# One issuer instead of two for the first loads, and inputs laid out by tile and by chunk

## The chip, the cores and the metric

The kernel runs on one core of one Trainium2 chip. The metric is the device time of one execution in microseconds (us). The core has a matrix engine (TensorE, PE in the rows, its weight loads PEld), a vector engine (VectorE, DVE), a scalar engine (ScalarE, ACT), GpSimd (POOL) and SyncE (SP), which here only issues transfers. ACT can issue transfers too. Each of the two issuers has a queue of its own (q1 is SP's, q10 is ACT's), and both are served by the same 16 DMA engines.

## The reference

`x` is 16 batches of 128 x 128. A mixture of experts with a shared expert is added to it (8 routed experts, D = 128, F = 512), and then one matrix per batch, picked from a table of 100 by `fwd_steps`, is applied and added.

```python
g = jnp.einsum('bsd,edf->ebsf', h, Wg)
u = jnp.einsum('bsd,edf->ebsf', h, Wu)
expert_outs = jnp.einsum('ebsf,efd->ebsd', jax.nn.silu(g) * u, Wd)
expert_output = jnp.einsum('be,ebsd->bsd', gating_probs, expert_outs)
shared = jnp.einsum('bsf,fd->bsd', jax.nn.silu(h @ Sg) * (h @ Su), Sd)
sg = shared_gate_prob[:, :, None]
x = x + (1.0 - sg) * expert_output + sg * shared
x = x + jnp.einsum('bij,bjk->bik', T[fwd_steps - 1], x)
```

## The kernel before

The work is cut into steps. A step is one expert (9 with the shared one), one tile of 512 columns (4 batches; there are `NT` = 4 tiles) and one chunk of 128 of the 512 hidden features (`NC` = 4 chunks): 144 steps. Float32 accuracy is had by splitting each operand into a rounded high part and a low part (`x_hi`/`x_lo`, `w_hi`/`w_lo`, `h_hi`/`h_lo`) and adding three matmuls for each product. So a step has nine matmuls of 128 x 512: three for `g_bank` and three for `u_bank` (L378 to L380), and, two steps later (`LAG`), three for `o_bank` (L404, L405, L407). ACT takes `silu` of `g_bank` (L236) and rounds `h` (L242), DVE multiplies by `u_bank` (L295) and makes `h_lo` (L301). POOL splits the weights of the next expert (L168, L173) and adds the scaled results to `acc` (L218). Every engine has its program written out by hand; semaphores link them.

`w_raw` holds two experts (two slots). The first expert is loaded in parts, so that work can begin before all of it is there. In memory its row for a partition is 4 chunks of gate, up and down weights, 128 floats each. The start goes like this:

- SP issues tile 0 of `x` into `acc` (256 KB), then gate and up of chunks 2 and 3 (L132, 256 KB), then down of all four chunks (L133, 256 KB), then tile 1 of `x`, `side`, tiles 2 and 3 of `x`, and the second expert (L126, 768 KB).
- ACT issues gate and up of chunk 0 and of chunk 1 (L258, 128 KB each), `wc0_in[0]` and `wc0_in[1]` being their semaphores. Then it loads its table for silu and waits for the chunks in turn, rounding each (L255).
- DVE rounds tile 0 of `x` as soon as it is there (L329) and makes `x_lo` of it (L331), then `w_lo` of chunk 1 (L333), then rounds chunks 2 and 3 (L336).
- POOL makes `w_lo` of chunk 0, then of chunks 2 and 3, then of the down weights (all L168).
- PE runs six matmuls on zeros (L432), waits for `x_hi` and chunk 0, and runs the high products of chunk 0 and, once it is rounded, of chunk 1 (L438). Only then come the low products of both chunks (L441, L442), and then the steps from the third on, one behind the other. `project_down` of step 0 (L404) needs the low part of the down weights.

From the second expert on, a whole expert is loaded into the slot that POOL has just freed.

Of the kernel before, what the change touches and what calls it, by code (L numbers as in the profile page):

```python
# [12 lines left out]
def moe_then_step_kernel(  # L13
# [8 lines left out]

    S, B, D = out.shape
    E = W_all.shape[0] - 1
    NC = W_all.shape[2]
    K = TT.shape[0]
    assert S == P and D == P
    BT = 4
# [1 line left out]
    W = BT * S  # L30
    U = NT * NC
    N_ROUTED = E * U
# [5 lines left out]
    EARLY = 3  # L38
    assert NC == 4 and NT == 4 and E % 2 == 0

    with ExitStack() as ctx:
        def sb(name, shape, dt=F32):
            return ctx.enter_context(nc.sbuf_tensor(name, shape, dt))

        def sem(name):
            return ctx.enter_context(nc.semaphore(name))
# [3 lines left out]
        x_lo = sb("x_lo", [P, NT, W], F32R)  # L50
        w_raw = sb("w_raw", [P, 2, NC, 3, P])
        w_hi = sb("w_hi", [P, 2, NC, 3, P], F32R)
        w_lo = sb("w_lo", [P, 2, NC, 3, P], F32R)
        silu_g = sb("silu_g", [P, 2, W])
# [3 lines left out]
        acc = sb("acc", [P, NT, W])  # L58
# [15 lines left out]
        wc0_in = [sem(f"wc0_in{i}") for i in range(3)]  # L74
        wd0_in = sem("wd0_in")
        w_in = [sem(f"w_in{s}") for s in range(2)]
# [27 lines left out]
        parts = [(t * BT, BT) for t in range(NT - 1)] + [((NT - 1) * BT + b, 1) for b in range(BT)]  # L104
        last_part = len(parts) - 1
        parts_of = [[i for i, (b, _) in enumerate(parts) if b // BT == t] for t in range(NT)]

        def part_bank(i):

            b, nb = parts[i]  # L110
            return o_bank[(b // BT) % 2] if nb == BT else u_bank[b % BT]
# [3 lines left out]

        SCALE = [N_ROUTED + NC * t + NC + LAG for t in range(NT - 1)]
        TURN = [n + 1 for n in SCALE]
# [5 lines left out]
        @block.sync  # L123
        def _(sp):
            def load_expert(slot, e):
                sp.dma_start(w_raw[:, slot, :, :, :], W_all[e, :, :, :, :].rearrange("a p c m f -> (a p) c m f")).then_inc(w_in[slot], 16)  # L126

            def load_x(t0, t1, s):
                sp.dma_start(acc[:, t0:t1, :], xT[:, t0:t1, :]).then_inc(s, 16)

            load_x(0, 1, x_in[0])
            sp.dma_start(w_raw[:, 0, 2:NC, 0:2, :], W_all[0, :, 2:NC, 0:2, :]).then_inc(wc0_in[2], 16)  # L132
            sp.dma_start(w_raw[:, 0, :, 2, :], W_all[0, :, :, 2, :]).then_inc(wd0_in, 16)  # L133
            load_x(1, 2, x_in[1])
            sp.dma_start(side_b[:, :], side).then_inc(c_in, 16)
            load_x(2, NT, x_in[2])
            load_expert(1, slice(1, 2))

            sp.wait_ge(split_done, EARLY)
            with sp.Fori(1, E // 2) as pair:  # L140
                for slot in range(2):

                    sp.wait_ge(w_ready, 2 * NC * pair + NC * (slot - 1))
                    load_expert(slot, bass.ds(2 * pair + slot, 1))

            with sp.Fori(0, B) as b:
                which = sp.value_load(step[bass.ds(b, 1)].rearrange("(a n) -> a n", a=1), min_val=1, max_val=K)
                sp.dma_start(T_plus[:, bass.ds(b, 1), :], TT[bass.ds(which - 1, 1), :, :].rearrange("n j i -> j n i")).then_inc(T_in, 16)
            sp.wait_ge(w_ready, NC * (E - 1))
            load_expert(0, slice(E, E + 1))  # L150


            for first, last in [(i, i) for i in range(NT - 1)] + [(NT - 1, NT), (NT + 1, NT + 2)]:
                b0, b1 = parts[first][0], parts[last][0] + parts[last][1]
                sp.wait_ge(res_done, last + 1)
                sp.dma_start(out[:, b0:b1, :], res[:, b0:b1, :]).then_inc(stored, 16)
            sp.wait_ge(stored, 16 * (NT + 1))
# [72 lines left out]
        @block.scalar  # L230
        def _(act):
            def silu(n, k):


                act.wait_ge(g_done, n + 1)
                nc.scalar.activation(silu_g[:, k % 2, :], g_bank[k % 2][:, :], ACT.Silu).then_inc(g_read, 1)  # L236

            def round_h(n, k):


                act.wait_ge(h_done, n + 1)
                nc.scalar.activation(h_hi[:, k % HR, :], u_bank[k % HR][:, :], ACT.Copy).then_inc(h_rounded, 1)  # L242

            def copy_y(i):
                b, nb = parts[i]
                act.wait_ge(y_turned, i + 1)
                nc.scalar.activation(y[:, b:b + nb, :], part_bank(i)[:, 0:nb * D].rearrange("p (b d) -> p b d", b=nb),
                                     ACT.Copy).then_inc(y_done, 1)

            def round_x(t):  # L250
                act.wait_ge(x_in[min(t, 2)], 16)
                nc.scalar.activation(x_hi[:, t, :], acc[:, t, :], ACT.Copy).then_inc(x_rounded, 1)

            def round_w0(c, m):
                nc.scalar.activation(w_hi[:, 0, c, m, :], w_raw[:, 0, c, m, :], ACT.Copy).then_inc(w0_rounded, 1)  # L255

            for c in range(2):
                act.dma_start(w_raw[:, 0, c, 0:2, :], W_all[0, :, c, 0:2, :]).then_inc(wc0_in[c], 16)  # L258
            act.wait_ge(zero_done, 1)
            nc.scalar.activation(silu_0[:, :], zero[:, 0:1], ACT.Silu)  # L260
            for c in range(2):
                act.wait_ge(wc0_in[c], 16)
                round_w0(c, slice(0, 2))
            silu(0, 0)
            act.wait_ge(wd0_in, 16)
            round_w0(slice(0, NC), 2)
            silu(1, 1)
            round_h(0, 0)
            round_x(1)
            for n in range(2, PEEL_ACT):  # L270
                silu(n, n)
                round_h(n - 1, n - 1)

                if n >= PEEL_ACT - 2:
                    round_x(NT - PEEL_ACT + n)
            with act.Fori(0, N_ROUTED, U) as n0:
                for k in range(PEEL_ACT, U + PEEL_ACT):
                    silu(n0 + k, k)
                    round_h(n0 + k - 1, k - 1)
            for n in range(N_ROUTED + PEEL_ACT, N + 1):  # L280
                if n in COPY[:-1]:
                    copy_y(COPY.index(n))
                if n < N:
                    silu(n, n)
                round_h(n - 1, n - 1)
            for i in range(NT - 2, len(parts)):
                copy_y(i)
# [244 lines left out]
```

## Time and profile before

| | |
|---|---|
| median of 3 runs | 311.44 us (311.27 to 313.25) |
| the profiled execution | 311.43 us |
| its span, from the first to the last instruction | 309.6 us |
| around the span (the difference) | 1.83 us |
| PE busy | 303.3 us, 98% of the span |
| DVE, ACT, POOL busy | 214.0, 163.5, 102.5 us |
| granted TensorE clock, mean | 0.998 |
| moved by DMA | 10.39 MB, mean 34 GB/s |

The span is what the trace shows; the time outside it is not seen there. PE is busy nearly throughout, so the places to look at are the few microseconds in which it is not.

### The profile page before, as it was taken

What the parts mean: (1) busy time and instruction counts of PE and PEld (TensorE: products, weight loads), DVE (VectorE), ACT (ScalarE), POOL (GpSimd) and SP (SyncE); (2) the same over time, 40 slices, a digit from 0 to 9 for tenths busy, and PEclk for the clock granted to TensorE, in tenths of its full rate; (3) what the DMA queues carried; (4) which work ended last, traced back from release to release, by engine and by line L of the source; (5) the groups of instructions that cost most, each with busy time, mean ns of one, the idle gap of its engine ahead of it and who ended that gap; (6) DMA issues with size and microseconds to landing.
All of it is one profiled execution on the core that took longest, in us unless ns stands there. A gap on an engine that the chain in (4) does not pass through costs nothing.

```text
span 309.6 us, 4555 instructions
## 1 busy us (share of the span) xinstructions
PE 303.3 (98%) x1356; PEld 251.1 (81%) x1356; DVE 214.0 (69%) x348; ACT 163.5 (53%) x303; POOL 102.5 (33%) x116
## 2 busy tenths in 40 slices
PE   5999999999999999999999999999999999999995
PEld 4788888888888888888888888888888888888884
DVE  2667766777667666677766776667766676667785
ACT  2765555555555555555555555555555555554552
POOL 2675213441145115511551144312441155180000
PEclk9999999999999999999999999999999999999999
DMA  7600300020003000110003000012000000000011
GB/s 216 233 2 0 103 1 2 0 102 1 0 0 95 6 0 0 28 74 0 0 0 111 25 25 25 25 37 90 0 0 0 0 0 0 0 2 0 34 36 68
DMA packets 5847, 10.39 MB, mean 34 GB/s; under 512 B 592, under 2 KB 4048, under 8 KB 5840
## 3 DMA queue, kind: packets, MB, share of 16 engines
q1 hardware_dynamic: 5552, 10.04, 9.7%
q10 hardware_dynamic: 288, 0.26, 0.3%
q8 instruction: 4, 0.07, 0.1%
q14 instruction: 3, 0.02, 0.0%
HBM read 9.25 MB, written 1.05 MB: 33 GB/s over the span
## 4 chain that ended last, share of the span: by engine, by line
PE 97%; DMA 2%; DVE 0%; ACT 0%; ACTq 0%; issue 0%
PE o_bank L404 11%; PE o_bank L405 11%; PE o_bank L407 11%; PE g_bank L378 10%; PE u_bank L378 10%; PE g_bank L379 10%; PE u_bank L379 10%; PE g_bank L380 10%; PE u_bank L380 10%; DMA w_raw<-in_W_all 2%; PE o_bank L425 1%; PE o_bank L417 0%; DVE res L324 0%; PE u_bank L417 0%; PE g_bank L438 0%; PE g_bank L441 0%
## 5 line engine op out<-in xcount | busy, mean ns | idle before, releaser
L295 DVE TENSOR_TENSOR u_bank<-u_bank,silu_g 128x512 f32<-128x512 f32 x144 | 100.8, 700 | 85.9 <-PE u_bank L380 84.2
L236 ACT ACTIVATE silu_g<-g_bank 128x512 f32<-128x512 f32 x144 | 86.1, 598 | 133.8 <-PE g_bank L380 132.3
L301 DVE TENSOR_TENSOR h_lo<-u_bank,h_hi 128x512 fp32r<-128x512 f32 x144 | 98.0, 681 | 0.1
L218 POOL TENSOR_TENSOR acc<-acc,scaled 128x512 f32<-128x512 f32 x32 | 41.4, 1295 | 163.2 <-DVE scaled L309 163.0
L242 ACT ACTIVATE h_hi<-u_bank 128x512 fp32r<-128x512 f32 x144 | 85.5, 594 | 0.7 <-DVE u_bank L295 0.7
L404 PE MATMUL o_bank<-h_hi,w_hi 128*128 128x512 f32 x144 | 56.2, 391 | 0.0
L407 PE MATMUL o_bank<-h_lo,w_hi 128*128 128x512 f32 x144 | 56.1, 389 | 0.0
L405 PE MATMUL o_bank<-h_hi,w_lo 128*128 128x512 f32 x144 | 56.0, 389 | 0.0
L378 PE MATMUL g_bank<-x_hi,w_hi 128*128 128x512 f32 x142 | 55.6, 392 | 0.0
L380 PE MATMUL g_bank<-x_hi,w_lo 128*128 128x512 f32 x142 | 55.3, 389 | 0.0
L378 PE MATMUL u_bank<-x_hi,w_hi 128*128 128x512 f32 x142 | 55.3, 389 | 0.0
L379 PE MATMUL g_bank<-x_lo,w_hi 128*128 128x512 f32 x142 | 55.3, 389 | 0.0
L380 PE MATMUL u_bank<-x_hi,w_lo 128*128 128x512 f32 x142 | 55.2, 389 | 0.0
L379 PE MATMUL u_bank<-x_lo,w_hi 128*128 128x512 f32 x142 | 55.2, 389 | 0.0
L168 POOL TENSOR_TENSOR w_lo<-w_raw,w_hi 128x384 fp32r<-128x384 f32 (+2 forms) x36 | 36.3, 1011 | 7.8 <-ACT w_hi L255 4.6
L404 PEld LDWEIGHTS o_bank<-h_hi,w_hi 128*128 128x128 f32 x144 | 27.0, 188 | 5.8 <-POOL w_lo L168 0.3
L407 PEld LDWEIGHTS o_bank<-h_lo,w_hi 128*128 128x128 f32 x144 | 27.0, 188 | 5.8
L405 PEld LDWEIGHTS o_bank<-h_hi,w_lo 128*128 128x128 f32 x144 | 27.0, 188 | 5.5
L380 PEld LDWEIGHTS g_bank<-x_hi,w_lo 128*128 128x128 f32 x142 | 26.7, 188 | 5.6
L380 PEld LDWEIGHTS u_bank<-x_hi,w_lo 128*128 128x128 f32 x142 | 26.7, 188 | 5.6
L378 PEld LDWEIGHTS u_bank<-x_hi,w_hi 128*128 128x128 f32 x142 | 26.7, 188 | 5.6
L379 PEld LDWEIGHTS u_bank<-x_lo,w_hi 128*128 128x128 f32 x142 | 26.7, 188 | 5.5
(51 smaller groups left out, 145.2 us busy)
## 6 DMA issues: line engine op xcount, KB each, us to landing
w_raw<-in_W_all SPq DMA_DIRECT2D x8, 768.0 KB, 4.4
T_plus<-in_TT SPq DMA_DIRECT2D x16, 64.0 KB, 1.7
out_y<-res SPq DMA_DIRECT2D x3, 256.0 KB, 2.5
acc<-in_xT SPq DMA_DIRECT2D x2, 256.0 KB, 5.0
w_raw<-in_W_all SPq DMA_DIRECT2D x2, 256.0 KB, 5.4
acc<-in_xT SPq DMA_DIRECT2D x1, 512.0 KB, 6.0
w_raw<-in_W_all ACTq DMA_DIRECT2D x2, 128.0 KB, 4.9
out_y<-res SPq DMA_DIRECT2D x2, 128.0 KB, 2.4
```

Source lines behind the costliest of these rows:

```text
L168: return nc.gpsimd.tensor_tensor(w_lo[:, slot, c, m, :], w_raw[:, slot, c, m, :], w_hi[:, slot, c, m, :].bitcast(F32), ALU.subtract)
L218: nc.gpsimd.tensor_tensor(acc[:, t, :], acc[:, t, :], scaled[:, t % 2, :], ALU.add).then_inc(acc_done, 1)
L236: nc.scalar.activation(silu_g[:, k % 2, :], g_bank[k % 2][:, :], ACT.Silu).then_inc(g_read, 1)
L242: nc.scalar.activation(h_hi[:, k % HR, :], u_bank[k % HR][:, :], ACT.Copy).then_inc(h_rounded, 1)
L295: nc.vector.tensor_tensor(u_bank[k % HR][:, :], u_bank[k % HR][:, :], silu_g[:, k % 2, :], ALU.mult).then_inc(h_done, 1)
L301: nc.vector.tensor_tensor(h_lo[:, k % HR, :], u_bank[k % HR][:, :], h_hi[:, k % HR, :].bitcast(F32), ALU.subtract).then_inc(split_done, 1)
L378: nc.tensor.matmul(bank, w_hi[:, w[0], w[1], w[2], :], x_h, start=start, stop=False)
L379: nc.tensor.matmul(bank, w_hi[:, w[0], w[1], w[2], :], x_l, start=False, stop=False)
L380: return nc.tensor.matmul(bank, w_lo[:, w[0], w[1], w[2], :], x_h, start=False, stop=stop)
L404: nc.tensor.matmul(o_bank[t % 2][:, :], w_hi[:, w[0], w[1], w[2], :], h_hi[:, slot, :], start=c == 0, stop=False)
L405: nc.tensor.matmul(o_bank[t % 2][:, :], w_lo[:, w[0], w[1], w[2], :], h_hi[:, slot, :], start=False, stop=False)
L407: last = nc.tensor.matmul(o_bank[t % 2][:, :], w_hi[:, w[0], w[1], w[2], :], h_lo[:, slot, :], start=False, stop=c == NC - 1)
```

## The change

All loads of the start are now issued by SP, and chunk 0 and chunk 1 stand right behind tile 0 of `x`; ACT issues none. The arrays have another order in memory: `x` is stored as four tiles of 128 x 512, each contiguous (before, a partition's row held all four tiles, 8 KB, and a tile took 2 KB of each row). The weights of an expert are stored as four chunks, each 128 rows of gate, up and down (1.5 KB a row); before, a partition's row held all four chunks (6 KB). In the scratchpad nothing moves.

```diff
-    NC = W_all.shape[2]
+    NC = W_all.shape[1]
...
             def load_expert(slot, e):
-                sp.dma_start(w_raw[:, slot, :, :, :], W_all[e, :, :, :, :].rearrange("a p c m f -> (a p) c m f")).then_inc(w_in[slot], 16)
+                sp.dma_start(w_raw[:, slot, :, :, :], W_all[e, :, :, :, :].rearrange("a c p m f -> p (a c) m f")).then_inc(w_in[slot], 16)
 
             def load_x(t0, t1, s):
-                sp.dma_start(acc[:, t0:t1, :], xT[:, t0:t1, :]).then_inc(s, 16)
+                sp.dma_start(acc[:, t0:t1, :], xT[t0:t1, :, :].rearrange("t p w -> p t w")).then_inc(s, 16)
 
             load_x(0, 1, x_in[0])
-            sp.dma_start(w_raw[:, 0, 2:NC, 0:2, :], W_all[0, :, 2:NC, 0:2, :]).then_inc(wc0_in[2], 16)
-            sp.dma_start(w_raw[:, 0, :, 2, :], W_all[0, :, :, 2, :]).then_inc(wd0_in, 16)
+            sp.dma_start(w_raw[:, 0, 0, 0:2, :], W_all[0, 0, :, 0:2, :]).then_inc(wc0_in[0], 16)
+            sp.dma_start(w_raw[:, 0, 1, 0:2, :], W_all[0, 1, :, 0:2, :]).then_inc(wc0_in[1], 16)
+            sp.dma_start(w_raw[:, 0, 2:NC, 0:2, :], W_all[0, 2:NC, :, 0:2, :].rearrange("c p m f -> p c m f")).then_inc(wc0_in[2], 16)
+            sp.dma_start(w_raw[:, 0, :, 2, :], W_all[0, :, :, 2, :].rearrange("c p f -> p c f")).then_inc(wd0_in, 16)
...
-            for c in range(2):
-                act.dma_start(w_raw[:, 0, c, 0:2, :], W_all[0, :, c, 0:2, :]).then_inc(wc0_in[c], 16)
             act.wait_ge(zero_done, 1)
...
     def pack(gate, up, down):
         e = gate.shape[0]
-        g = gate.reshape(e, P_, NC_, P_)
-        u = up.reshape(e, P_, NC_, P_)
-        d = down.reshape(e, NC_, P_, P_).transpose(0, 2, 1, 3)
+        g = gate.reshape(e, P_, NC_, P_).transpose(0, 2, 1, 3)
+        u = up.reshape(e, P_, NC_, P_).transpose(0, 2, 1, 3)
+        d = down.reshape(e, NC_, P_, P_)
         return _np.stack([g, u, d], axis=3)
...
-        "xT": x.transpose(2, 0, 1).reshape(D_, 4, -1),
+        "xT": x.transpose(2, 0, 1).reshape(D_, 4, -1).transpose(1, 0, 2),
```

SP, from its first instruction to its loop over the experts, before. `in_xT` and `in_W_all` are the arrays in memory, `acc` and `w_raw` the tiles they go to:

```order
1 L129 DMA acc<-in_xT 128x512
2 L132 DMA w_raw<-in_W_all 128x2x256
3 L133 DMA w_raw<-in_W_all 128x4x128
4 L129 DMA acc<-in_xT 128x512
5 L135 DMA side_b<-in_side 128x144
6 L129 DMA acc<-in_xT 128x1024
7 L126 DMA w_raw<-in_W_all 128x1536
```

The same stretch of SP after the change:

```order
1 L129 DMA acc<-in_xT 128x512
2 L132 DMA w_raw<-in_W_all 128x256
3 L133 DMA w_raw<-in_W_all 128x256
4 L134 DMA w_raw<-in_W_all 128x2x256
5 L135 DMA w_raw<-in_W_all 128x4x128
6 L129 DMA acc<-in_xT 128x512
7 L137 DMA side_b<-in_side 128x144
8 L129 DMA acc<-in_xT 128x2x512
9 L126 DMA w_raw<-in_W_all 128x4x384
```

Two issues of 128 x 256 stand ahead of the rest, which keeps its order; an expert is now 128 x 4 pieces of 384 floats instead of 128 of 1536, and tiles 2 and 3 of `x` are two pieces a partition instead of one.

ACT, from its start, before:

```order
0 L230 UNCONDITIONAL_BRANCH
1 L258 DMA w_raw<-in_W_all 128x256 x2
2 L260 ACT_TABLE_LOAD
3 L260 ACTIVATE silu<-zero 128x1
4 L255 ACTIVATE w_hi<-w_raw 128x256 x2
```

ACT, after:

```order
0 L232 UNCONDITIONAL_BRANCH
1 L260 ACT_TABLE_LOAD
2 L260 ACTIVATE silu<-zero 128x1
3 L257 ACTIVATE w_hi<-w_raw 128x256 x2
4 L238 ACTIVATE silu_g<-g_bank 128x512
```

Only the two issues are gone from ACT. The instructions of PE, DVE and POOL are the same and in the same order.

## Rows read from the trace of the kernel before

**Rows 1.** The page: span, and busy time and share of PE.

```profile
span 309.6 us, 4555 instructions
PE 303.3 (98%) x1356; PEld 251.1 (81%) x1356; DVE 214.0 (69%) x348; ACT 163.5 (53%) x303; POOL 102.5 (33%) x116
```

**Rows 2.** The chain that ended last, 0 to 14 us: start, length, what.

```profile
0.74 0.41 ACTq L258
...
1.18 5.15 DMA w_raw<-in_W_all
...
6.35 0.43 ACT w_hi L255
...
6.82 0.50 PE g_bank L438
...
10.76 0.35 PE o_bank L404
```

**Rows 3.** Timeline of SP's queue, start: start, length, line.

```profile
0.74 0.39 SPq L129 DMA_DIRECT2D acc<-in_xT  x1
1.19 0.42 SPq L132 DMA_DIRECT2D w_raw<-in_W_all  x1
1.65 0.64 SPq L133 DMA_DIRECT2D w_raw<-in_W_all  x1
```

**Rows 4.** Timeline of ACT, DVE, POOL and PE to 11 us; in brackets, idle time before.

```profile
5.36 0.42 ACT L255 ACTIVATE w_hi<-w_raw 128x256 fp32r<-128x256 f32 x1 [2.20 <-DMA w_raw<-in_W_all]
8.55 0.62 ACT L255 ACTIVATE w_hi<-w_raw 128x512 fp32r<-128x512 f32 x1
10.02 0.64 ACT L252 ACTIVATE x_hi<-acc 128x512 fp32r<-128x512 f32 x1
...
5.17 0.43 DVE L329 CAST x_hi<-acc 128x512 fp32r<-128x512 f32 x1 [4.16 <-DMA acc<-in_xT]
...
5.86 1.05 POOL L168 TENSOR_TENSOR w_lo<-w_raw,w_hi 128x256 fp32r<-128x256 f32 x1 [4.38 <-ACT w_hi L255]
...
1.06 2.93 PE L432 MATMUL o_bank<-zero 128*128 128x128 f32 x12 [1.06 <-DVE zero L327]
5.92 0.47 PE L438 MATMUL g_bank<-x_hi,w_hi 128*128 128x512 f32 x1 [1.93 <-ACT w_hi L255]
7.38 0.40 PE L441 MATMUL g_bank<-x_lo,w_hi 128*128 128x512 f32 x1
```

**Rows 5.** Issues from 1.6 to 1.7 us: KB, median us to landing.

```profile
w_raw<-in_W_all SPq DMA_DIRECT2D x2, 256.0 KB, 5.4
```

**Rows 6.** Queues from 2 to 4 us, then 9 to 10: packets, MB, share of 16 engines.

```profile
q1 hardware_dynamic: 112, 0.21, 59.9%
q10 hardware_dynamic: 89, 0.09, 14.8%
...
q1 hardware_dynamic: 67, 0.37, 89.5%
```

**Rows 7.** Windows: length, PE, PEld, DVE, ACT, POOL, PEclk, DMA share, GB/s.

```profile
2.00:3.00 1.00, 1.00 (x7) 1.00 (x6) 0.00 (x0) 0.99 (x2) 0.00 (x0) 1.00 0.83 158
3.00:4.00 1.00, 0.99 (x5) 0.70 (x4) 0.00 (x0) 0.16 (x1) 0.00 (x0) 1.00 0.67 134
4.00:5.00 1.00, 0.00 (x0) 0.00 (x0) 0.00 (x0) 0.00 (x0) 0.00 (x0) 1.00 1.03 352
5.00:6.00 1.00, 0.08 (x1) 0.11 (x1) 0.80 (x2) 0.42 (x1) 0.14 (x1) 1.00 1.14 366
...
33.00:34.00 1.00, 1.00 (x6) 0.84 (x5) 0.54 (x1) 0.80 (x2) 0.00 (x0) 1.00 0.74 184
34.00:35.00 1.00, 1.00 (x6) 0.81 (x5) 1.00 (x3) 0.25 (x1) 0.00 (x0) 1.00 0.98 395
```

**Rows 8.** A later expert load: its issue, and POOL's first use of it.

```profile
31.91 0.34 SPq L126 DMA_DIRECT2D w_raw<-in_W_all  x1
...
52.98 0.51 POOL L173 CAST w_hi<-w_raw 128x384 fp32r<-128x384 f32 x1
```

## The prediction

> **What bounds the kernel now.** I read the page first [rows 1]: PE is busy for 303.3 of 309.6 us, so only some 6 us of the span can be had from anything but PE's own work, and the change leaves that work alone. The chain of waits [rows 2] says where those microseconds are. From 6.82 us on it is PE behind PE, except for one place: the first `o_bank` matmul takes 0.35 us of the chain instead of the 0.23 of its neighbours. Before 6.82 it goes back over ACT's rounding of chunk 1 to the transfer of chunk 1, issued at 1.18 us and 5.15 us under way. So the start is bound by loads, the other 302 us by PE. What the change gives or takes is how much earlier or later the unbroken run of PE begins; everything behind slides with it.
>
> The timeline [rows 4] shows the start. PE's matmuls on zeros are over at 3.99 us. `x_hi` waits for `x` until 5.17. ACT starts to round chunk 0 at 5.36, so it landed at about 5.27, PE starts at 5.92, and the pair of high products of chunk 1 at 6.82 (chunk 1 landed at 1.18 + 5.15 = 6.33). The low products begin at 7.38.
>
> **What a start needs.** Call the landing of chunk 0 A and of chunk 1 B. Two paths lead to the low products:
> - by chunk 1: B + 1.05 (7.38 - 6.33): rounding 0.42, two matmuls and the steps between.
> - by POOL's `w_lo` of chunk 0, which takes 1.05 and ended at 5.86 + 1.05 = 6.91 [rows 4], 1.64 behind A; with 0.05 to pass it on, A + 1.69. Before that was 6.96 and hidden under 7.38.
> The later of the two counts. `x` adds 0.43 + 0.69 for its high and low parts behind its landing and is hidden as long as it lands no later than A.
>
> **The change part by part.**
>
> *Issue.* An issue on SP takes 0.39 to 0.42 us, and the next starts 0.45 us behind it [rows 3]. Chunk 0 goes out at 1.19 instead of 0.74, chunk 1 at 1.64 instead of 1.18, chunks 2 and 3 and the down weights 0.9 later (2.1 and 2.55). This costs time only where a transfer would else have been moving data in those 0.45 us. By 4.0 the DMA engines are far behind what was issued (0.30 MB moved [rows 6] of the 1.05 MB of the first five loads), so the later issue is hidden by the backlog. Without that cover it costs 0.45 us at B and A.
>
> *Order in the queue.* Bytes moved, from the windows [rows 7]: 0.30 MB by 4 us, 0.35 MB more by 5, 0.37 MB more by 6, so 0.65 MB at 5.0 and 1.02 at 6.0. At A = 5.27 it was 0.75 MB, at B = 6.33 it was 1.14 MB. `x` and chunk 0 are 0.39 MB, with chunk 1 0.52 MB. So 0.36 MB of later loads (chunks 2 and 3, down) had been moved by A and 0.62 MB by B: two queues share the engines, and SP's brings what is needed later. In one queue these stand behind. Full credit, at 360 GB/s: A 1.0 earlier (4.3), B 1.7 earlier (4.6). The sum goes to max(4.3 + 1.69, 4.6 + 1.05) = 5.99, a gain of 1.4 us. Little credit: by 4.0 most of `x` (0.21 of 0.26 MB) had been moved, yet it landed at about 5.1; so some engines are late with `x` itself, and what stands behind it on those is not helped by the order. Then A stays near `x` at 5.1 and B follows at 128 KB behind it, 0.4 us, 5.5: max(6.79, 6.55) = 6.8, a gain of 0.6.
>
> *Layout of `x`.* From 2 to 4 us q1 moved 112 packets in 59.9% of 16 engines, 171 ns each, most of them of 2 KB. From 9 to 10 us, 67 packets with 0.37 MB (6 KB each, but for a few) took 89.5%, 214 ns each, so 71 ns for 2 KB [rows 6]. The first `x` is read at well under half speed. Whether its pitch of 8 KB in memory does that, the trace doesn't say directly. An expert load, which is one contiguous block before, is also slow at its start, 184 GB/s, but one microsecond later it runs at 395 [rows 7]; `x` and the chunks stay at 134 to 158 for two. If the contiguous `x` shortens the slow time to that of an expert load (which is issued at 31.91 and runs at its full rate from 34.0, 2.1 us later, with 0.18 MB moved), then the same from 0.74 gives 0.18 MB at 2.8, 0.39 MB at 3.4 and 0.52 MB at 3.7 us. For the engines that lag I add 0.5, half of the 1.1 us from 4.0, when most of `x` had been moved, to its landing. A is 3.9 and B 4.2, the low products begin at 5.6, and the gain is 1.8. It cannot be much more, since PE's zeros end at 3.99. If the pitch has no part in it, the gain is the 0.6 to 1.4 above. Below nothing there is no reason for a contiguous tile to go.
>
> I take A = 4.5 and B = 4.9: the order in the queue gets most of its credit, and part of the slow time goes. That is nearest to the row of 134 GB/s, which is slower than anything that an expert load shows. Low products at max(4.5 + 1.69, 4.9 + 1.05) = 6.19, against 7.38: **1.2 us gained**.
>
> *What comes next in line.* When PE starts 1.2 us earlier, its next needs do too. Chunks 2 and 3 are third in the queue, at 0.79 MB: 5.4 at the old rate, and DVE comes to them at about 5.9. The down weights landed at 1.65 + 5.4 = 7.05 [rows 3, 5], ACT took them at 8.55 [rows 4], now at 7.35; they lie at the same 1.05 MB of the stream as before, with nothing between, so they land no later than 7.05. The stall of 0.12 at the first `o_bank` matmul is POOL's, on a chain that hangs on `silu` of step 0 and so slides with PE: unchanged. Tile 1 of `x` is used at 10.02, now 8.8; its bytes are through at 1.31 MB, 6.8 us, and even 1 us behind that is early enough.
>
> *Weights in four pieces.* An expert load is 512 pieces of 1.5 KB instead of 128 of 6 KB. On SP, the load with 512 pieces took 0.64 us to issue against 0.34 for one with 128 [rows 3, 8]: 0.3 us eight times, on an engine that does nothing but wait then. The transfer, issued at 31.91, is first used at 52.98 [rows 8]: 21 us for a transfer that takes under 5, so even twice as long it is hidden. If that cover were gone, PE would stall once per expert for the excess. Zero.
>
> *ACT* is rid of two issues, 0.41 us the first [rows 2], ahead of its table load. It then waits 2.2 us for chunk 0 [rows 4]: zero.
>
> The Trainium skill (DMA: Bandwidth & Descriptors, "Issuing engines are not separate DMA queues") speaks against the change: issuing from several engines saves the issuing time, and all DMAs run on the same 16 engines anyway. By it alone, moving ACT's two issues to SP only adds 0.45 us. The trace is at odds with taking it so: what the second queue moves comes out of the same 16 engines, and 0.62 MB of later data went ahead of chunk 1.
>
> **Sum.** Profiled execution: span 309.6 - 1.2 = 308.4, with 1.83 around it 310.2. It stands at 311.43, 0.01 under the median of 311.44, so the median becomes 310.2.
>
> **Rivals.**
> 1. *`x` was slow because of its pitch* and now runs like an expert load: gain 1.6 to 2 (1.8 by the working above), 309.4 to 309.8. For it: 171 ns per packet against 71. Against: a contiguous expert load starts slowly too. The Trainium skill (same page, "Anatomy of one DMA") gives a fixed 2.0 us and the bytes at 436 GB/s, measured for another way of issuing; by its figures `x` would land at 3.3 us and the result be near this rival. This trace has 5.1 for it, so I give it no more than its rows do.
> 2. *Each load has its own latency from issue to landing* and the order in the queue doesn't matter: chunk 0 took 4.5, chunk 1 5.15, the two of SP 5.4 [rows 2, 4, 5], nearly the same whatever stood ahead. Then chunk 1 lands at 1.64 + 5.15 = 6.8, the low products begin 0.45 later, and the time is **311.9, slower**. It decides as soon as the order saves chunk 1 less than the 0.45 us by which it is issued later. Against it: the latencies grow from 4.5 to 5.4 with place, and 352 to 366 GB/s from 4 us on is a stream at its limit.
> 3. *It doesn't do what it says*: the slow stretch is a matter of one queue fed by one issuer, and in FIFO the engines idle where ACT's packets had filled in. Then what the order saves is lost there: 311.1 to 311.6.
>
> **How the numbers follow.** Forecast (gain 0.6 to 1.5): 0.53. Rival 1: 0.22. Rival 3: 0.12. Rival 2: 0.10. Other, such as a late down weight or a disturbed median: 0.03. The predicted time is that of the first. The range takes the forecast, rival 1 and rival 3 whole, 309.4 to 311.5, with rival 2 outside; the first and last tenth of a microsecond are for the medians. One per cent is 3.1 us, about what a measurement of this kernel can tell from no change. Faster by that would need PE at work before its zeros end: 0.01. Slower by that needs a late expert load, which the 21 us exclude but for something unseen: 0.02. Within: 0.97.
>
> **What would show it.** On the changed profile: DVE's `x_hi` starts at 4.2 to 4.5 instead of 5.17; ACT rounds chunk 0 at about 4.6 and chunk 1 right behind, with hardly an idle gap; the chain before the low products no longer passes by chunk 1's transfer but by POOL's `w_lo` of chunk 0; they begin at about 6.2; from there to the end nothing differs but the offset. q1 alone moves data. Wrong would be: `x` still at 5.1, chunk 1 behind 6, or a new wait of PE at chunks 2 and 3 or at the down weights.

## The result

The changed kernel takes 310.36 us in the median of 20 executions (309.76 to 312.22); before, 20 executions beside them had a median of 312.69. The ratio is 0.994, 95% interval 0.9925 to 0.9956: 1.9 us less, 1.4 to 2.3. The profiled execution took 310.24 with a span of 308.4, against 311.43 and 309.6 [rows 1].

The page of the changed kernel. PE is as busy as before, for a shorter span:

```profile
span 308.4 us, 4555 instructions
PE 303.6 (98%) x1356; PEld 251.2 (81%) x1356; DVE 213.9 (69%) x348; ACT 163.3 (53%) x303; POOL 102.3 (33%) x116
```

The chain that ended last, start of the changed kernel (start, length, what):

```profile
1.66 3.58 DMA w_raw<-in_W_all
...
5.25 0.42 ACT w_hi L257
...
5.72 0.50 PE g_bank L438
...
9.65 0.35 PE o_bank L404
```

It has the shape of [rows 2], 1.1 us earlier: still chunk 1's transfer, ACT's rounding, and PE behind PE. It is issued 0.48 later and is 3.58 under way instead of 5.15. The timeline of DVE, ACT, POOL and PE answers to [rows 4]:

```profile
3.25 0.43 DVE L329 CAST x_hi<-acc 128x512 fp32r<-128x512 f32 x1 [2.25 <-DMA acc<-in_xT]
...
3.54 0.42 ACT L257 ACTIVATE w_hi<-w_raw 128x256 fp32r<-128x256 f32 x1 [1.31 <-DMA w_raw<-in_W_all]
5.25 0.42 ACT L257 ACTIVATE w_hi<-w_raw 128x256 fp32r<-128x256 f32 x1 [1.29 <-DMA w_raw<-in_W_all]
...
4.04 0.95 POOL L170 TENSOR_TENSOR w_lo<-w_raw,w_hi 128x256 fp32r<-128x256 f32 x1 [2.56 <-ACT w_hi L257]
...
4.11 0.76 PE L438 MATMUL g_bank<-x_hi,w_hi 128*128 128x512 f32 x1
6.29 0.39 PE L441 MATMUL g_bank<-x_lo,w_hi 128*128 128x512 f32 x1
```

`x` is there at 3.2 instead of 5.1, chunk 0 at 3.45 instead of 5.27; the first products, at 4.11, now come right behind PE's zeros, which are over at 3.99. But ACT then idles 1.29 us for chunk 1. The low products begin at 6.29 instead of 7.38. The windows (length, PE, PEld, DVE, ACT, POOL, PEclk, DMA share, GB/s) show the transfers, beside [rows 7]:

```profile
2.00:3.00 1.00, 1.00 (x7) 1.00 (x6) 0.00 (x0) 0.23 (x2) 0.00 (x0) 1.00 0.96 322
3.00:4.00 1.00, 0.99 (x5) 0.69 (x4) 0.71 (x2) 0.42 (x1) 0.00 (x0) 1.00 0.94 189
4.00:5.00 1.00, 0.90 (x2) 0.50 (x2) 0.41 (x1) 0.00 (x0) 0.95 (x1) 1.00 0.75 221
```

Twice the rate of before in the first of these microseconds, while `x` moves, and then a slow stretch while the chunks move. In its first microsecond the DMA engines are busy (0.94), so there it is their packets that take long; in the second they are partly idle (0.75).

The executions of before fall into two groups. Of 96 executions of it, in four series beside the kernels of this study (one more, at 627 us, is left out), 8 lie at 311.3 to 311.6 and 88 at 312.2 to 313.9. The profiled one at 311.43 is of the small group. The changed kernel has 13 of 20 at 309.8 to 310.7 and 7 at 311.9 to 312.2. What the groups are is the second question of the experiments.

The twelve kernels below were measured in three series (e1 to e4, e5 to e8, e9 to e12), each on another chip and beside executions of before of its own (medians 313.05, 312.79, 312.91). Each ratio is against those; kernels of different series are best compared by their ratios.

### The profile page after: what moved, and what is told of

Read it like the earlier page. It is cut to its first block, busy times and chain, and to the rows that moved or that the text cites. A ratio compares the mean times of both kernels' runs of the same rounds, so it can differ in the third digit from the quotient of the medians.

```text
span 308.4 us, 4555 instructions
## 1 busy us (share of the span) xinstructions
PE 303.6 (98%) x1356; PEld 251.2 (81%) x1356; DVE 213.9 (69%) x348; ACT 163.3 (53%) x303; POOL 102.3 (33%) x116
## 3 DMA queue, kind: packets, MB, share of 16 engines
q1 hardware_dynamic: 9040, 10.30, 10.8%
## 4 chain that ended last, share of the span: by engine, by line
PE 97%; DMA 1%; DVE 0%; SPq 0%; ACT 0%; issue 0%
PE o_bank L404 11%; PE o_bank L407 11%; PE o_bank L405 11%; PE g_bank L380 10%; PE u_bank L380 10%; PE g_bank L379 10%; PE u_bank L379 10%; PE g_bank L378 10%; PE u_bank L378 10%; DMA w_raw<-in_W_all 1%; PE o_bank L425 1%; PE o_bank L417 0%; DVE res L324 0%; PE u_bank L417 0%; PE g_bank L438 0%; PE g_bank L442 0%
```

## The experiments

Theory P: the old layout of `x` made its load slow. Theory Q: the two queues did, and one queue in order of need mends it. The first four kernels take the change apart.

**Only the layout of `x`** (e1_x_tiles):

```diff
-                sp.dma_start(acc[:, t0:t1, :], xT[:, t0:t1, :]).then_inc(s, 16)
+                sp.dma_start(acc[:, t0:t1, :], xT[t0:t1, :, :].rearrange("t p w -> p t w")).then_inc(s, 16)
```

(The host code stores `x` as the change does.)

> Only the layout of x is changed; weights and issuers are as before. If the pitch of 8 KB made the first x slow (theory P), x lands at 3.2 to 3.8 us although ACT's queue moves beside it, and the time falls by 0.6 to 1.5 us. If the sharing of the engines by two queues made it slow (theory Q), x still lands at 4.8 to 5.1 and the time stays within 0.3 us of before.

Median 311.91 (310.04 to 312.46), ratio 0.995 (0.9931 to 0.9969). `x` took 3.4 us from issue to landing instead of 4.4, chunk 1 landed at 5.3 instead of 6.3. The queues from 2 to 4 us (packets, MB, share of 16 engines), beside 0.21 and 0.09 MB [rows 6]:

```profile
q1 hardware_dynamic: 288, 0.40, 53.7%
q10 hardware_dynamic: 191, 0.18, 26.6%
```

Twice the bytes with both queues at work: P.

**Only the layout of the weights** (e2_w_chunks), with the issuers of before:

```diff
-                sp.dma_start(w_raw[:, slot, :, :, :], W_all[e, :, :, :, :].rearrange("a p c m f -> (a p) c m f")).then_inc(w_in[slot], 16)
+                sp.dma_start(w_raw[:, slot, :, :, :], W_all[e, :, :, :, :].rearrange("a c p m f -> p (a c) m f")).then_inc(w_in[slot], 16)
...
-                act.dma_start(w_raw[:, 0, c, 0:2, :], W_all[0, :, c, 0:2, :]).then_inc(wc0_in[c], 16)
+                act.dma_start(w_raw[:, 0, c, 0:2, :], W_all[0, c, :, 0:2, :]).then_inc(wc0_in[c], 16)
```

(The other two loads of the first expert are addressed in the same way, and the host code stores the weights as the change does.)

> Only the layout of the weights is changed; x and issuers are as before. Both theories: x lands at about 5 us as before and the low products begin within 0.3 us of 7.38, so no change in time (within 0.3 us). An expert load of 512 pieces lands up to 1 us later and PE does not wait for it.

Median 313.27, ratio 1.0007 (0.9995 to 1.0019): nothing. `x` took 4.9 us to land, even a little longer. The 0.4 us of chunk 1 behind before's (6.77 against 6.33) is a single execution's; in it the low products began at 7.93, more than the 0.3 us behind 7.38 that was expected. The 512 pieces per expert cost PE nothing.

**Only the order** (e3_sp_order), with both layouts of before:

```diff
             load_x(0, 1, x_in[0])
+            for c in range(2):
+                sp.dma_start(w_raw[:, 0, c, 0:2, :], W_all[0, :, c, 0:2, :]).then_inc(wc0_in[c], 16)
...
-            for c in range(2):
-                act.dma_start(w_raw[:, 0, c, 0:2, :], W_all[0, :, c, 0:2, :]).then_inc(wc0_in[c], 16)
```

> Only the issuer and the order are changed: SP issues chunk 0 and chunk 1 behind x; both layouts are as before. Theory Q: all or nearly all of the gain, x lands at 3.2 to 4.2, chunk 1 at 4.6 to 5.3, and the low products begin at about 6.3, 1.0 to 1.5 us off the time. Theory P: x still lands at 4.7 or later, chunk 1 at 5.5 or later, gain 0 to 0.6 us.

Median 312.1 (310.71 to 313.84), ratio 0.9968 (0.9946 to 0.9991). Between the two expectations: `x` landed in 4.0 us, chunk 0 at 5.04, and chunk 1 so soon behind it that ACT rounded the two back to back. The windows have the slow rate of before although only one queue is at work:

```profile
2.00:3.00 1.00, 1.00 (x7) 1.00 (x6) 0.00 (x0) 0.23 (x2) 0.00 (x0) 1.00 0.64 183
3.00:4.00 1.00, 0.99 (x5) 0.69 (x4) 0.00 (x0) 0.00 (x0) 0.00 (x0) 1.00 0.77 158
```

So one queue doesn't cure the slow `x`, though it lands 0.4 us sooner than in before's trace; mainly it keeps chunk 1 from being overtaken by the later loads (landed before 5.5 instead of at 6.33). The gain, 1.0 us by the ratio, is more than the 0.6 that P allowed.

**Both layouts, the issuers of before** (e4_layouts): the edits of e1_x_tiles and e2_w_chunks together.

> Both layouts are changed, the issuers are as before (ACT issues chunks 0 and 1). Theory P: x lands at 3.2 to 3.8 and most of the gain is here, except for what chunk 1 loses to SP's later loads: low products at 6.3 to 6.9. Theory Q: low products at 7.1 or later, within 0.3 us of before.

Median 311.54 (310.20 to 312.19), ratio 0.9951 (0.9934 to 0.9969). `x` landed in 3.2 us and chunk 1 at 5.18; the profiled execution's span is 308.4, that of the changed kernel. P again. Chunk 1 lands no later with ACT's queue than in one queue (5.24), though SP's later loads move beside it. `x` and chunk 0 do land later: `x` takes 3.2 instead of 2.5 us, and ACT comes to chunk 0 at 4.22 instead of 3.54. The slow stretch of the changed kernel (189 and 221 GB/s) is absent:

```profile
3.00:4.00 1.00, 0.99 (x5) 0.69 (x4) 0.00 (x0) 0.17 (x1) 0.00 (x0) 1.00 1.06 379
4.00:5.00 1.00, 0.22 (x1) 0.25 (x2) 0.95 (x2) 0.42 (x1) 0.28 (x1) 1.00 1.11 356
```

The bytes moved from 2 to 4 us sort all profiled kernels by the layout of `x` alone: 0.29 MB (before), 0.32 (e2), 0.34 (e3) with the old one; 0.51 (changed), 0.58 (e1), 0.58 (e4) with the new. The later kernels keep to it: 0.30 and 0.34 with the old, 0.41 to 0.65 with the new. Within the new layout the issuer matters too. With SP alone (changed, e6, e7) `x` took 2.5 to 2.7 us, and from 3 to 5 us 0.35 to 0.41 MB moved. With ACT issuing as well (e1, e4, e8, e9, e10, e12) `x` took 3.0 to 3.4 us, and 0.60 to 0.74 MB moved in the same two microseconds. So one queue brings `x` earlier and then meets a slow stretch, in all three traces with it; the six with two queues don't show one.

**The clock.** The profiled execution of e1_x_tiles took 312.25, though chunk 1 was 1 us early. Its chain says why:

```profile
4.40 0.42 ACT w_hi L255
...
4.96 0.77 PE g_bank L438
5.73 0.43 PE u_bank L438
...
9.60 0.43 PE u_bank L441
10.03 0.26 PE u_bank L442
10.29 0.23 PE g_bank L378
```

Matmuls of 512 columns follow each other at 0.43 us until 10.0, which is the clock's lower level (512 / 1.2 GHz = 0.427), and at 0.23 from there. Eleven of them at 0.2 us too much are 2.2 us, more than the 1 us by which chunk 1 was early. The column of the granted clock shows 1.00 there; only the spacing tells. In e2_w_chunks (313.24) the column shows it too:

```profile
6.00:7.00 1.00, 0.62 (x2) 0.30 (x2) 0.74 (x2) 0.44 (x2) 0.68 (x1) 1.00 1.13 385
...
8.00:9.00 1.00, 1.00 (x4) 0.81 (x3) 0.01 (x1) 0.00 (x0) 0.91 (x2) 0.50 1.02 382
...
11.00:12.00 1.00, 1.00 (x6) 0.84 (x5) 0.49 (x1) 1.00 (x3) 0.49 (x1) 0.94 0.02 8
```

Full, then half from 7.7 on, then full again. PE had paused from 4.0 to 6.4. The record of before's executions has such a drop too: of the 73 of the larger group whose mean granted clock is on record, 16 show 0.994 or 0.995, as this execution of e2 does (0.995); the four of the small group show 0.998. Theory C: the two groups of executions differ in how long the clock is at its lower level at the start, and the pause of PE between its zeros and its first products puts it there. The rival L: they differ in their loads. The next four kernels were made for this, the last of them also for chunk 1.

**Before, with more zeros** (e5_before_zeros10):

```diff
-            warm_up(6)
+            warm_up(10)
```

> The kernel before with ten matmul calls on zeros instead of six, so that PE is busy until about 5.7 us instead of 3.99; loads and order are as before. Theory C (most executions of the kernel before lose 1 to 2 us more than its profiled one because PE's clock is at its lower level for part of the start, after the pause between the zeros and the first products): the time falls by 0.8 to 2 us from the median of before, towards 311.4, with the loads unchanged. Rival L (the executions differ by their loads): no change, within 0.3 us.

Median 311.48, 11 of 12 executions from 311.29 to 311.64; ratio 0.9959 (0.9945 to 0.9973). In the same series 26 of 29 executions of before lay above 312.2. Loads are those of before (chunk 0 at 5.27). Four more calls on zeros take 1.3 us off the median, with the loads unchanged: the groups come from what PE does, as C says, and not from the loads. But the clock still rises late in its profiled execution, after three products at the lower level:

```profile
6.61 0.43 PE u_bank L438
7.04 0.41 PE g_bank L438
7.45 0.23 PE u_bank L438
```

PE had been busy from 1.06 on with no pause above 0.2 us, so here no pause put the clock at its lower level: it had not risen yet. The zeros say the same. In e9_layouts_busy and e11_order_busy four matmuls on zeros stand between the high pairs, in e9 with the upper level reached and in e11 not:

```profile
4.84 0.43 PE g_bank L438
5.26 0.41 PE u_bank L438
5.68 0.44 PE o_bank L432 x4
6.12 0.23 PE g_bank L438
```

```profile
6.39 0.43 PE u_bank L438
6.81 0.85 PE o_bank L432 x4
7.67 0.43 PE g_bank L438
```

One takes 0.11 us at the upper level and 0.21 at the lower. The twelve at the start of before took 2.93 us, 0.24 each [rows 4], and in every trace with more than one call the early ones stand 0.21 apart. So every execution traced begins at the lower level, and what differs is when the clock rises. C has the clock right. But in these traces the pause doesn't lower it, except in e2; at most it puts off the rise. In before's profiled execution the clock rose within its pause of 1.9 us, since the products behind it stand at 0.23 from the first.

**The changed kernel, PE kept busy** (e6_after_busy):

```diff
-            warm_up(6)
+            warm_up(8)
...
                 high(u_bank[c][:, :], c, 1)
+                if c == 0:
+                    warm_up(2)
```

> The changed kernel with eight calls on zeros instead of six, and two more between the pairs of high products of chunks 0 and 1, where PE idles. Theory C: the executions at 312.0 of the changed kernel become rare, median 310.0 to 310.4 with little spread, 0.992 of before or lower. Rival L: as the changed kernel, part of the executions at 312, ratio about 0.994.

Median 310.54, 0.14 above the expected range, all five executions from 310.19 to 310.75, none at 312; ratio 0.993 (0.9913 to 0.9947). Against e5_before_zeros10 (311.48), both with PE kept busy, the change of loads is worth 0.9 us; part of that may be the clock, which in the profiled executions was up before the first product here and only after three in e5. The profiled execution shows what comes next in line. Chunk 1 landed early (ACT at 4.87), the low products began at 5.92, but the 0.4 us were given back at chunks 2 and 3 and at the down weights:

```profile
4.87 0.42 ACT L257 ACTIVATE w_hi<-w_raw 128x256 fp32r<-128x256 f32 x1 [0.66 <-DMA w_raw<-in_W_all]
...
5.92 0.39 PE L441 MATMUL g_bank<-x_lo,w_hi 128*128 128x512 f32 x1
...
9.11 0.39 PE L380 MATMUL u_bank<-x_hi,w_lo 128*128 128x512 f32 x1
9.72 0.50 PE L404 MATMUL o_bank<-h_hi,w_hi 128*128 128x512 f32 x1 [0.22 <-POOL w_lo L170]
```

Its chain goes by the transfer of chunks 2 and 3 (issued at 2.13, 4.33 under way), DVE's rounding and POOL: the next bound of the start, 0.4 us behind the first.

**The changed kernel with one call on zeros** (e7_after_zeros1): `warm_up(1)` in place of `warm_up(6)`.

> The changed kernel with one call on zeros instead of six; loads and order are those of the changed kernel. Theory C: PE's first products run at 0.43 us each instead of 0.23 for some 3 to 7 us, so 1.5 to 3 us slower than the changed kernel, at 312.0 to 313.3: as much as the change gains, or more. Rival L: as the changed kernel, ratio about 0.994.

Median 311.38 (310.81 to 312.78), ratio 0.9965 (0.9951 to 0.998): 1 us slower than the changed kernel, not the 1.5 to 3 expected. The direction is C's, and the lower level is seen (products at 0.43 from the first one, at 4.32, until 10.8 in an execution of 312.71), but the size was missed: eight of the twelve executions lie at 310.8 to 311.5. They are not traced; that the clock came up earlier in them is argued from the time.

**Chunk 1 by ACT** (e8_act_chunk1):

```diff
-            sp.dma_start(w_raw[:, 0, 1, 0:2, :], W_all[0, 1, :, 0:2, :]).then_inc(wc0_in[1], 16)
...
+            act.dma_start(w_raw[:, 0, 1, 0:2, :], W_all[0, 1, :, 0:2, :]).then_inc(wc0_in[1], 16)
             act.wait_ge(zero_done, 1)
```

> The changed kernel, but ACT issues chunk 1 at 0.74 us beside SP's x and chunk 0. If late issue and place in the queue set chunk 1's landing (5.2 in the changed kernel), it lands at 3.6 to 4.5, x and chunk 0 at most 0.4 later, low products at about 5.7, up to 0.6 us less than the changed kernel. If engines that lag in any queue set it, chunk 1 lands at 4.8 to 5.4 and the time is that of the changed kernel within 0.3 us.

Median 311.6, ratio 0.9959 (0.9944 to 0.9975), slower than the changed kernel's 0.994 by its middle though the intervals overlap. `x` took 3.2 us, chunk 0 landed at 4.33, and ACT rounded the two chunks back to back. But the first products, from 4.92, ran at 0.43 us each until 9.0, and the low ones began at 6.76, not at 5.7. PE had paused for 0.9 us instead of 0.1. The loads question had to be asked with PE kept busy, which the last four do, each with the two edits of e6_after_busy.

**Both layouts, issuers of before, PE busy** (e9_layouts_busy):

> Both layouts changed, issuers as before (ACT issues chunks 0 and 1), and PE kept busy as in e6_after_busy (eight calls on zeros and two between the high pairs). If the layout of x gives nearly all of what the loads give (theory P), this is at 310.2 to 310.7, equal to e6_after_busy at 310.54. If one queue in order is needed (theory Q), 311.0 or more.

Median 310.45 (310.14 to 311.38), ratio 0.993 (0.9906 to 0.9953): equal to e6_after_busy. That doesn't show that the queues are of no account, because the loads no longer hold the start here: the chain goes back over the added zeros (L432, sixteen matmuls from 1.06 to 4.84) and not to a transfer, and the first two products run at the lower level. That of e6 does end at a transfer.

**Chunk 1 by ACT, PE busy** (e10_act1_busy):

> The changed kernel with chunk 1 issued by ACT and PE kept busy as in e6_after_busy. The slow clock took 1.9 us from e8_act_chunk1; without it the low products begin at 5.9 to 6.1, bound by POOL's low part of chunk 0, and the time is 310.0 to 310.4, the least of all. If chunks 2 and 3 are late next, it stays at 310.5.

Median 310.6 (310.20 to 311.02), ratio 0.9927 (0.9906 to 0.9949): no better than the others. The low products began at 6.67, not at 5.9 to 6.1; the chain goes back over the zeros here too.

**Only the order, PE busy** (e11_order_busy):

> Only issuer and order changed, both layouts as before, and PE kept busy as in e6_after_busy. Against e5_before_zeros10 (311.48, the loads of before with PE busy). Theory P: 311.0 to 311.5, the order gives under 0.5. Theory Q: 310.4 to 310.8.

Median 312.72, in two groups: five executions at 310.96 to 311.13, seven at 312.68 to 313.21; ratio 0.997 (0.9949 to 0.9991). This missed both expectations, since with the old `x` (4.0 us to land) eight calls on zeros don't reach: PE pauses for 0.8 us until 5.62, and in the profiled execution (312.94) its products run at 0.43 us each, until 9.8. What can be read is the lower group, of which no execution was traced: 0.4 us under e5_before_zeros10 and 0.3 under the small group of before (311.4). That is in P's range for the order.

**Only the layout of `x`, PE busy** (e12_x_busy):

> Only the layout of x changed, issuers and weights as before, and PE kept busy as in e6_after_busy. Theory P: 310.3 to 310.8, 0.7 to 1.2 under e5_before_zeros10 at 311.48. Theory Q: 311.2 or more.

Median 310.32 (310.13 to 311.32), ratio 0.9928 (0.9905 to 0.9952), 1.2 us under e5_before_zeros10 (1.0 by the ratios) and not above e6_after_busy. Its windows:

```profile
2.00:3.00 1.00, 1.00 (x7) 1.00 (x6) 0.00 (x0) 0.99 (x2) 0.00 (x0) 1.00 0.85 297
3.00:4.00 1.00, 1.00 (x7) 1.00 (x7) 0.13 (x1) 0.16 (x1) 0.00 (x0) 1.00 1.01 353
```

With two queues at work there is no slow stretch. With PE kept busy the layout of `x` alone gives all that the loads of the whole change give; this chain too goes back over the zeros. No kernel with the new `x` and PE kept busy can be told from the changed one by the medians (310.3 to 310.6 against 310.36); what they have is that the executions at 312 are gone.

## Why the prediction was right or wrong

**The time and the sum** came out: 310.2 forecast, 310.36 measured, span 308.4 forecast and found, the low products at 6.19 forecast and 6.29 found. The stage was right: only the start moved, and the stall of the first `o_bank` matmul slid along unchanged (0.35 us). Between the kernels with PE kept busy the loads gave 0.9 (e6) to 1.2 us (e12) where 1.2 was forecast, with a share for e5's late clock in it.

**The terms inside were both off and cancelled,** so that the number came out this close is luck. I took A = 4.5 and B = 4.9; they were 3.45 and 5.24. *Layout of `x`* was mis-sized: I gave it a part of the slow time, nearest to the row of 134 GB/s, and it took away most: alone it brings `x` in 3.4 us instead of 4.4 (e1). One queue on top makes it 2.5, with 322 GB/s between 2 and 3 us. Rival 1 had that mechanism and the better A (3.9). *Order in the queue* was mis-sized the other way. I let chunk 1 follow chunk 0 by 0.4 us; it took 1.8, because the chunks themselves ran into a slow stretch (189 and 221 GB/s). So the path by POOL, which I expected to decide, was hidden, and the chain still passes by chunk 1's transfer; there the profile contradicts what I wrote under what would show it.

**The credit for the order** went to the wrong place. With the old layout it gives 0.3 us (e11's lower group) to 1.0 (e3's ratio), around the 0.6 of my little-credit bound. With the new one it doesn't bring chunk 1 earlier: 5.24 in one queue, 5.18 in two (e4), and both profiled executions have a span of 308.4. What I counted as gained by chunk 1 from the order belongs to the layout. The two edits mend the same wait, so their gains don't add. With the new layouts SP alone does bring `x` and chunk 0 some 0.7 us earlier (ACT comes to chunk 0 at 3.54 against 4.22 in e4), and with them PE's first products (4.11 against 4.78 in e4). That may be worth something by the clock: with the new `x` and ACT's queue 5 of 20 executions lie under 311 (e1, e4), in the changed kernel 13 of 20. They come from different series, and the ratios of e4 (0.9951) and of the changed kernel (0.994) have overlapping intervals, so this is not shown.

One reading was off too: an expert load has moved 0.23 MB when it reaches its full rate at 34.0, not 0.18, because 49 GB/s had run from 32 to 33 us. It touches only rival 1, by 0.1 us.

**Rival 2** (own latencies, slower by 0.45) fell: chunk 1 was issued 0.48 later and landed 1.1 earlier, and in e3, with the old layouts, 0.45 later and over 0.8 earlier. **Rival 3** (the engines idle in one queue) lost on the time, and for the first stretch by 322 GB/s in one queue; but its mechanism is seen from 3 to 5 us, where one queue moved 0.35 to 0.41 MB and two 0.60 to 0.74, with the engines busy for as little as 0.49 (e7, 4 to 5 us). I had given it no part in the sum. The rule of the Trainium skill (DMA: Bandwidth & Descriptors, "Issuing engines are not separate DMA queues") that all issuers' transfers run on the same 16 engines turns out a fair guide to the time with the changed layouts: e4's profiled execution and the changed kernel's have the same span.

**Costed at zero and right:** the weights in four pieces (e2, 1.0007). ACT's freed time, SP's later issues and tile 1 of `x` have no run of their own; the changed profile has no wait of PE on any of them.

**What the prediction lacked is a term.** I set the profiled execution, 311.43, equal to the median of three. It is of a group that holds 8 of 96 executions; the usual time before is 312.9. Between the lower groups of before (311.4) and of the changed kernel (310.1) lie 1.3 us, close to the forecast 1.2, and between the upper ones (312.9 and 312.0) 0.9. The rest of the measured 1.9 comes from the change making the good group the common one, 13 of 20. That before's groups hang on what PE does is shown by e5, and that the clock is what differs by the slow products in the traces of e1, e2, e3, e7, e8 and e11 and by the granted clock of 16 executions; no execution of before's larger group was traced. For the changed kernel e6 has only five executions; together with e9, e10 and e12, which have medians like it, 23 of 23 lie at 311.4 or lower. Why the share rises is argued: the products start at 4.11, right behind the zeros, instead of after a pause of 1.9 us.

**Left open:** whether it is the pitch of 8 KB or the 1 MB over which the old tile was spread that made it slow; both left together, and no run separates them. Why the chunks meet a slow stretch in one queue (189 GB/s, and in e6 and e7) and in none of the six traces with ACT's queue beside it is open too, and so is what decides when the clock rises.

## What to carry to other kernels

Try the first load that the start waits for as one contiguous block; here that was worth more than who issues it and in what order. Read the spacing of the matmuls in the first microseconds, and the spread of the executions, before taking a profiled execution for the typical one: a clock that is not up yet at the first products can cost more than the load that PE waits for (2.2 us against 1 in e1), and here a warm-up that reaches to the first products made that rare. Where two edits relieve the same wait, try each alone; the second may be free to leave out.

## What the runs showed of the hardware

- The granted-clock column read 1.00 over a stretch in which 512-column matmuls stood at 0.43 us (e1_x_tiles, 5 to 10 us). Where the clock fell inside the trace (e2_w_chunks), it read 0.50.
- Every trace with six or more calls on zeros begins at the lower level: the early 128-column matmuls stand 0.21 us apart, against 0.11 at the upper one (e6, e9, e10, e12). With six calls on zeros and then a pause, the products ran at the upper level from the first one behind 0.8 (e4) and 1.9 us (before), and at the lower level from the first one until 9 to 10 us behind 0.9 to 1.6 us (e1, e3, e8); so did those of e11 behind eight calls and 0.8 us. Behind 2.4 us (e2) they began at the upper level and fell to the lower 1.3 us later. With PE kept busy without such a pause (e5, e6, e9, e10, e12) the upper level came at 7.45 us at the latest. So zeros followed by a pause make a late rise likely, not certain. The Trainium skill (TensorE: Matmul & The Clock Gate, "What's actually happening") describes a gate with two levels that follows how busy the array has been; the two spacings, 0.43 and 0.23, agree with two levels.
- A tile of 256 KB in 2 KB rows 8 KB apart took 4.0 to 4.9 us from issue to landing as a first load, the same tile in one block 2.5 to 2.7 with SP alone issuing and 3.0 to 3.4 with ACT issuing beside it.
